# Two transformer layers on one core: attention output written straight to its place, inverses spread by the matmul engine, row maxima first in the DMA queue, and the output product kept behind the last value product

## The reference

```python
xn = layernorm(x)
x = x + attn0(xn) + swiglu_ffn(xn)        # 32 heads of 16, one shared K and V, no mask, biases
xn = layernorm(x)
x = x + attn1(xn) + lora_moe_ffn(xn)      # 32 heads of 16, 8 K/V heads, rotary, causal
# each attention:
scores = einsum('bqhd,bkhd->bhqk', q, k) / 4
out = einsum('bhqk,bkhd->bqhd', softmax(scores), v).reshape(B, N, 512)
return out @ Wo
```

## Time and profile before

| | |
|---|---|
| three runs, median (lowest, highest) | 2288.86 us (2284.86, 2290.49) |
| the profiled execution | 2291.59 us |
| its span in the trace | 2289.9 us |
| PE, DVE, ACT, POOL busy | 2002.2, 1434.8, 1090.0, 227.9 us |
| attention of layer 0, first to last value product | about 530 to 1293.8 us |
| from there to the end of layer 1's router products | 1293.8 to 1399.8 us |
| attention of layer 1, from its first maxima | 1570.7 to 2219.5 us |
| from there to the end | 2219.5 to 2289.9 us |

### The profile page before, as it was taken

The page is one execution under the profiler, slowest core; times in us unless marked ns, Lnnn a source line. Parts: engine busy times, 40 slices in busy tenths (PEclk is TensorE's granted clock), DMA queues, the critical chain, the costliest instruction groups (busy, mean ns, idle before and its releaser), DMA issues.

```text
span 2289.9 us, 28931 instructions
## 1 busy us (share of the span) xinstructions
PE 2002.2 (87%) x10608; PEld 990.4 (43%) x10608; DVE 1434.8 (63%) x1876; ACT 1090.0 (48%) x2150; POOL 227.9 (10%) x603
## 2 busy tenths in 40 slices
PE   3999999999999999999988868997888888886668
PEld 3878787633333333333332355444333333332216
DVE  7443445328888888888774183396666656664424
ACT  3221212234777777777664421142555555554460
POOL 4000000000000000000010030000231313131130
PEclk7999999997999999999896689996998989897889
DMA  5010100151121111113110211033111111112113
GB/s 171 14 42 0 38 0 0 38 149 31 28 50 30 27 44 34 30 33 84 27 48 3 66 46 51 19 104 86 26 30 40 37 32 36 34 44 61 47 47 113
DMA packets 83297, 105.19 MB, mean 46 GB/s; under 512 B 18816, under 2 KB 52608, under 8 KB 83168
## 3 DMA queue, kind: packets, MB, share of 16 engines
q1 hardware_dynamic: 83168, 103.49, 17.5%
HBM read 72.50 MB, written 30.15 MB: 45 GB/s over the span
## 4 chain that ended last, share of the span: by engine, by line
PE 68%; DVE 10%; ACT 8%; SPq 6%; DMA 5%; issue 2%; POOL 0%; DVEq 0%; POOLq 0%; ACTq 0%
PE ps L1165 17%; PE ps L1194 11%; ACT arena L666 6%; PE ps L955 6%; PE ps L956 6%; PE ps L957 6%; PE ps L1190 6%; PE ps L1112 5%; PE ps L1073 4%; PE ps L1118 3%; DMA slots<-arena 3%; PE ps L1029 2%; DVE arena L891 2%; SPq L353 2%; SPq L350 2%
## 5 line engine op out<-in xcount | busy, mean ns | idle before, releaser
L891 DVE TENSOR_REDUCE arena<-ps 128x1 f32<-128x1024 f32 (+7 forms) x1024 | 976.4, 988 | 323.1 <-PE ps L1115 225.8
L666 ACT ACTIVATE arena<-ps 128x512 f32<-128x512 f32 (+3 forms) x1792 | 874.2, 555 | 526.2 <-PE ps L1190 293.2
L1165 PE MATMUL ps<-arena 128*17 128x512 f32 (+3 forms) x3584 | 455.2, 581 | 22.5 <-ACT arena L657 21.9
L1194 PE MATMUL ps<-slots 50*128 50x512 f32 x1024 | 397.2, 473 | 29.7 <-ACT arena L666 10.9
L1118 PE MATMUL ps<-slots 48*128 48x512 f32 x1024 | 414.4, 484 | 8.1 <-DVE arena L891 7.2
L1194 PEld LDWEIGHTS ps<-slots 50*128 50x128 f32 x1024 | 177.5, 195 | 351.4 <-ACT arena L666 280.1
L1190 PE MATMUL ps<-slots 98*128 98x512 bf16 (+3 forms) x768 | 230.5, 356 | 87.9 <-DMA slots<-arena 84.6
L1112 PE MATMUL ps<-slots 96*128 96x512 bf16 (+3 forms) x768 | 231.9, 361 | 20.2 <-DVE arena L891 7.0
L955 PE MATMUL ps<-x_hi,w_hi 128*128 128x512 f32 (+1 forms) x480 | 195.4, 407 | 56.9 <-DVE x_lo L921 35.7
L1118 PEld LDWEIGHTS ps<-slots 48*128 48x128 f32 x1024 | 174.5, 195 | 60.5 <-DVE arena L891 34.2
L523 POOL TENSOR_SCALAR_AFFINE_SELECT arena<-arena 128x128 f32<-128x128 f32 x512 | 146.9, 294 | 497.8 <-ACT arena L666 486.2
(11 more groups left out here) (119 smaller groups left out, 1719.6 us busy)
## 6 DMA issues: line engine op xcount, KB each, us to landing
slots<-qparts SPq DMA_DIRECT2D x96, 128.0 KB, 3.6
qparts<-arena SPq DMA_DIRECT2D x32, 256.0 KB
numer<-arena SPq DMA_DIRECT2D x256, 32.0 KB
xnT<-numer SPq DMA_DIRECT2D x16, 512.0 KB
arena<-inverse SPq DMA_DIRECT2D x16, 512.0 KB
slots<-qparts SPq DMA_DIRECT2D x96, 64.0 KB, 3.4
qparts<-arena SPq DMA_DIRECT2D x48, 128.0 KB
slots<-qparts SPq DMA_DIRECT2D x32, 192.0 KB, 3.7
```

Of the source, the lines that this page charges most:

```text
L666: act.activation(prob[local % P_RING][:, q0:CH], bank(local % SP_RING)[:, q0:CH], ACT.Exp, scale=SCALE).then_inc(S["p_ready"], 1)
L891: dve.tensor_reduce(maxes[c][:, h * TPC + qt:h * TPC + qt + 1], src[:, 0:max_width(l == 1, c, qt)], AX_X, ALU.max).then_inc(S["x_done"], 1)
L1165: mm = pe.matmul(bank(7)[32 * h:32 * h + DH + 1, q0:CH], v_slot[n % SLOTS][:, kt, :], prob[idx % P_RING][:, q0:CH], start=(kt == 0), stop= ...
L1194: mm = pe.matmul(bank(slot)[:, q0:CH], k_slot[u][r:r + ROWS[0] + MROWS, kt * P:(kt + 1) * P].bitcast(F32R), q_slot[u][r:r + ROWS[0] + MROW ...
```

## The change

Attention's results no longer go through DRAM. `store_o` copies each head's sums from `o_sb` into their place in `xnT`, and the sums of exponentials into `inv`, 32 heads times 4 rows of 128: 8 DMAs in place of 5. `load_output` and `load_inverses` are gone. A constant `sel` of zeros and ones lets PE spread the inverses over the 16 rows of each head (`broadcast`: four float32 products of 32 rows by 128 columns for each of 4 blocks `k` of a chunk). For batch 0 the eight broadcasts, with a DVE product `xnT *= ps` for each, stand among the maxima of group 13 (`norms`); ACT makes `xo_hi` in group 14 and POOL `xo_lo` in groups 14 and 15. `wo_hi` is made by ACT in group 10, `wo_lo` by POOL at the start of group 11. SP sends the maxima's rows of chunk 1 ahead of `load_slot`. In layer 0's last group the 11 items left are spread over the first 0.42 of it.

The output product has a list, `tail_ring`: tiles 0 to 5, the four broadcasts of chunk 2, tiles 6 to 8, those of chunk 3, tiles 9 to 15, in four banks (3 to 6). `FIRST_PROJ = 99` means that none of its steps is taken inside `attend`: all come behind the last value product. DVE follows with `evac`, `moments` and `normalise` in the order below. Layer 1's projection weights are loaded in group 2 of layer 0, its feed-forward weights right after the last `store_o`.

```diff
+LAST_MAX_END = [0.42, 0.0]
+FIRST_PROJ = [99, 99]
+STEPS_PER_QUAD = 3
+    return tiles[0:6] + norms[2] + tiles[6:9] + norms[3] + tiles[9:TT]
...
             def store_o(l, n, c):
                 S = L[l]
                 sp.wait_ge(S["o_copied"], n * QC + c + 2)
+                b = n // NG
                 for h in range(HG):
-                    sp.dma_start(numer[l][n * HG + h:n * HG + h + 1, :, c * CH:(c + 1) * CH].rearrange("o d q -> (o d) q"),
+                    head = n % NG * HG + h
+                    r = head % (P // DH) * DH
+                    sp.dma_start(xnT[r:r + DH, head // (P // DH), b * N + c * CH:b * N + (c + 1) * CH],
                                  o_sb[c][32 * h:32 * h + DH, :]).then_inc(S["o_out"][c], 16)
-                sp.dma_start(denom[l][n * HG:(n + 1) * HG, c * CH:(c + 1) * CH],
-                             o_sb[c][DH:P:32, :]).then_inc(S["o_out"][c], 16)
+                    sp.dma_start(inv[head * TPC:(head + 1) * TPC, b * QC + c, :],
+                                 o_sb[c][32 * h + DH:32 * h + DH + 1, :].rearrange("o (a q) -> o a q", q=P)).then_inc(S["o_out"][c], 16)
...
-                    if n == GROUPS - 4:
-                        load_output(l, 0)
-                    if n == GROUPS - 2:
-                        load_inverses(l, 0)
-                    final = n == GROUPS - 1
+                    max_rows(l, u, 1, n * QC + 1)
                     if n + SLOTS - 1 < GROUPS:
                         sp.wait_ge(S["pv_done"], n * group_quads[l] + PQ)
                         load_slot(l, n + SLOTS - 1)
-                    max_rows(l, u, 1, n * QC + 1)
                     store_o(l, n, 0)
...
+                        if (n, c) == (GROUPS - 5, 0):
+                            pool.wait_ge(S["wo_hi_done"], KC)
+                            pool.tensor_tensor(wo_lo[:, :, :], w_o[:, :, :], wo_hi[:, :, :].bitcast(F32), ALU.subtract).then_inc(S["wo_ready"], 1)
...
+                dve.wait_ge(S["pv_done"], (GROUPS - 1) * group_quads[l] + PQ)
+                evac(0, 4)
+                chunk_moments(0)
+                evac(4, 6)
+                invert(2, 3, GROUPS)
+                norm(2)
+                low(2)
+                invert(3, 4, GROUPS)
+                evac(6, 9)
+                norm(3)
+                evac(9, 10)
+                low(3)
+                evac(10, 12)
+                chunk_moments(1)
+                if l == 0:
+                    normalise(1, 0)
+                chunk_moments(2)
+                if l == 0:
+                    normalise(1, 1)
+                evac(12, 16)
+                if l == 0:
+                    normalise(1, 2)
+                chunk_moments(3)
+                if l == 0:
+                    normalise(1, 3)
...
+                def broadcast(dst, c, k):
+
+                    rows = slice(32 * k, 32 * (k + 1))
+                    for a in range(TPC):
+                        mm = pe.matmul(dst[:, a * P:(a + 1) * P], sel[rows, a, :], inv[rows, c, :], start=True, stop=True,
+                                       tile_position=(32 * k, 0))
+                    return mm
...
-                            steps = [0] * len(todo)
+                            steps = [a * LAST_MAX_END[l] for a in pace(todo)]
+                            tail_at = 0
...
+                                if not has_next and h == BURST_AT and i_g > HG * FIRST_PROJ[l]:
```

More of the change, by code:

```diff
@@ L82, in max_blocks @@
         before = [(n - 1, 1, None, None)] if n else []
-        blocks.append(r[0][:2] + before + r[0][2:] + r[1][:2] + [(n, 0, None, None)] + r[1][2:])
+        norms = [(None, c, None, k) for c in range(QC) for k in range(KC)] if n == GROUPS - 2 else []
+        blocks.append(r[0][:2] + before + norms + r[0][2:] + r[1][:2] + [(n, 0, None, None)] + r[1][2:])
     blocks[-1].append((B * NG - 1, 1, None, None))
@@ L89, in max_width, with norms_through, tail_ring @@
     return (TPC * qc + qt + 1) * P if causal else N
+def norms_through():
+    items = [item for block in max_blocks() for item in block]
+    return items.index((None, QC - 1, None, KC - 1)) + 1
+def tail_ring():
+    norms = [[("norm", c, k) for k in range(KC)] for c in range(NCH)]
+    tiles = [("tile", t // TPC, t) for t in range(TT)]
+    return tiles[0:6] + norms[2] + tiles[6:9] + norms[3] + tiles[9:TT]
 def build(nc, x, wq0, bq0, wk0, bk0, wv0, bv0, wo0, bo0, wgu, wdn, wq1, wk1, wv1, wo1,
@@ L144, in build @@
             x_lo = fb("x_lo", [P, 2, KC, CH], F32R)
-            wo_hi, wo_lo = x_hi[:, 0, :, :], x_hi[:, 1, :, :]
-            xo_hi = w_hi[:, :, :].rearrange("p n f -> p (n f)")[:, 0:2 * KC * CH].rearrange("p (i k q) -> p i k q", i=2, k=KC)
-            xo_lo = x_lo
             xn0 = fb("xn0", [P, XN_RING[0], D])
@@ L161, in build @@
             slots1 = fb("slots1", [P, 2 * SLOTS * SLOT], BF16)
-        AR = 25 * 1024
+        XO = P_RING * CH + QC * CH + NCH * P
+        with ExitStack() as own:
+            fb("below_xo", [P, XO])
+            xo_hi = fb("xo_hi", [P, 2, KC, CH], F32R)
+            xo_lo = fb("xo_lo", [P, 2, KC, CH], F32R)
+        XN1 = XO + 4 * KC * CH
+        AR = 26 * 1024
+        with ExitStack() as own:
+            fb("below_wo", [P, AR - 2 * KC * D])
+            wo_hi = fb("wo_hi", [P, KC, D], F32R)
+            wo_lo = fb("wo_lo", [P, KC, D], F32R)
         arena = sb("arena", [P, AR])
@@ L211, in build @@
         o_sb = [region(CH) for _ in range(QC)]
[L212 to L216 removed]
+        inv = region(NCH * P).rearrange("p (c q) -> p c q", c=NCH)
+        assert used[0] == XO
         used[0] = PROJECTION + SLOTS * SLOT
@@ L515, in _, with low @@
                     stage_v(n)
+                def low(c):
+                    pool.wait_ge(S["xo_hi_done"], KC * (c + 1))
+                    pool.tensor_tensor(xo_lo[:, c % 2, :, :], xnT[:, :, c * CH:(c + 1) * CH], xo_hi[:, c % 2, :, :].bitcast(F32),
+                                       ALU.subtract).then_inc(S["xo_ready"], 1)
                 at = 0
@@ L583, in _ @@
                 else:
-                    for t in range(TT):
-                        act.wait_ge(S["hl_ready"], t + 1)
-                        act.activation(hl[:, t, :], bank(t % 2)[:, 0:E * R + E], ACT.Copy).then_inc(S["hl_sb"], 1)
                     act.wait_ge(S["gap_done"], 1)
@@ L678, in _ @@
                 attend()
[L681 to L689 removed]
+                for c in range(QC, NCH):
+                    for k in range(KC):
+                        xo_high(c, k)
+                    if l == 0 and c == QC:
                         deviation(1, 0)
@@ L735, in _ @@
                 dve.wait_ge(x_in[g], 16)
+                moments(0, g)
                 normalise(0, g)
@@ L1213, in _ @@
                     max_piece(*piece)
-                attend()
+                for step in range(attend(), steps_in_all):
+                    tail_step(step)
                 pe.wait_ge(S["o_copied"], GROUPS * QC + 1)
-                pe.wait_ge(S["wo_ready"], 1)
-                for t in range(TT):
-                    c, q = t // TPC, slice(t % TPC * P, (t % TPC + 1) * P)
-                    pe.wait_ge(S["xo_ready"], c + 1)
-                    if t >= 8:
-                        pe.wait_ge(S["y2_evac"], t - 7)
-                    for k in range(KC):
-                        last = passes(bank(t % 8), xo_hi[:, c % 2, k, q], xo_lo[:, c % 2, k, q], wo_hi[:, k, :], wo_lo[:, k, :], k == 0, k == KC - 1)
-                    last.then_inc(S["y2_ready"], 1)
 def kernel(**inputs):
```

303 lines of the change are left out of this document (181 added, 122 removed).

## The result

| | before | changed |
|---|---|---|
| median of the runs, us | 2286.86 (2283.43 to 2290.49) | 2198.43 (2188.06 to 2203.94) |
| profiled execution, us | 2291.59 | 2201.31 |
| its span, us | 2289.9 | 2199.4 |
| ratio to before | | 0.961, 95% interval 0.957 to 0.965 |

The change gains 88 us where 141 were forecast, and the median lies 8 us above the range. Three lines of the changed kernel's page: busy time, the clock in 40 slices, the chain by engine.

What follows compares the result with a forecast made beforehand. PE holds 68% of the chain, so its waits and low clock bound the kernel. Terms 100.0 - 13.4 + 15.4 + 3.7 + 23 + 12 = 140.7 off 2291.6 give 2150.9, as a median 2148 us; range 2115 to 2190.

Steps and rivals of the forecast that it cites:

- Rows first: Layer 1's attention: sending the maxima's rows ahead of the next slot's loads removes waits and lost clock, gaining 100.0 us.
- the two long waits: Layer 1, groups 12 and 14: PE's longest waits on the rows, with batch 0's reading back also queued; 17.18 us at 2165.09.
- the new wait: Layer 1, groups 1 to 14: PE's remaining wait on the rows, taken as 0.25 us each, bounds 0 to 0.8.
- the rows still come late: Rival: the store's new DMAs cost 0.85 each, PE waits 2.8 us again and the clock falls; 2203 us, chance 0.12.
- The additions in layer 1: Layer 1's attention: broadcasts 6 us, POOL's `wo_lo` 5, ACT's copies 1, longer last store 1.4; together -13.4 us.
- Layer 0, groups 12 to 14: Layer 0's attention: 17.4 us go, less 4.7 for clock, 6.5 for broadcasts and norms, 2.5 for copies; gain 3.7 us.
- The third rival: Layer 0: the inserted work starves PE and the clock is low through groups 13 to 15; 2163 us, chance 0.10.
- The reading back: Layer 0, groups 12 to 14: reading back batch 0 cost 17.4 us, forecast to go.
- The charge for the clock behind the reciprocal: Layer 0, ahead of group 12's maxima: the reciprocal stays and PE's low clock just behind it costs 4.7 us again.
- The last group: Layer 0's last group: spreading the 11 items left gains 23 us, with nine quads at low clock; bounds 12 to 38.
- the first rival: Layer 0's last group: the clock stays high, 15.6 us less, 2132 us; chance 0.20.
- The ends: After the last value products: layer 0 to the router's last product gains 12 us (6 to 20), layer 1's end 15.4.

Runs made afterwards that it cites:

- ends and rows: Changed kernel with batch 0's broadcasts at the head of each layer's end and layer 1's second-chunk rows ahead of the stores; 2136.9 us, 0.932 of the kernel before.

## Why the prediction was wrong, and where it was right

**Rows first (100.0).** The mechanism and the size of what was removed are right: the swap alone brings 82 us with the two long waits left in. Wrong is the new wait: "I take 0.25, too short to lower the clock", from stores at 0.46 us an issue, the mean of the old five. The new ones take 0.62 with the gaps between them (4.93 for eight; 0.51 to 0.54 for an output of 16 partitions, 0.62 to 0.65 for a row of sums, where the rows of the kernel before had 0.43 and 0.55), which makes the rows 1.2 us later than forecast. That is beyond the bound too, which put 0.57 on each (and comes to 0.65 us of wait by its own rows, not 0.8). PE waits 18.8 us in all and not 3.5, and clock goes with it: 31 us by the kernel that takes the stores out of the way. The rival "the rows still come late" was this mechanism, with 0.12 and a threshold of 0.85; it set in well below that.

**The additions in layer 1 (-13.4).** The broadcasts' group takes 14 us too long, where 6 were charged: a broadcast between scores takes 1.12 us at the high clock and not 0.9 (four in one go in the tail take 2.8, 0.7 each), and the clock falls in the middle of the eight (0.53 from 2033 on), after which each takes 2.07. The 5 us for POOL's low half, with ACT's copies of the weight, are seen as 4 where no waits hide them (33.8 and 33.9 us for groups 10 and 11 against 31.9).

**Layer 0, groups 12 to 14 (3.7).** This is the step that failed most: "PE has hardly any idle time in a regular group, so 6.5 (0 to 9)". The broadcasts cost 30.3 us between two transposes and 33.4 over three half groups, where 9 were charged with ACT's copies. The bounds were made from their own duration at the high clock. Nothing was asked about what their place in the list does: the pacing makes room for them by crowding the maxima, whose bound is VectorE (1.18 us each); this crowding alone is 11.7. And nothing was asked about the clock: it falls while they run, also without the crowding (10 us of low clock; both effects together 37), and each then takes 2.07. The third rival came near (0.10), with a low clock, but by a starved PE, which the rows do not show, and let it cost 15 us in all. The reading back is gone as forecast. The charge for the clock behind the reciprocal was right: 5.5 us (27.4 for the half group at 1040.36) for the 4.7 forecast, though in four of the other kernels' profiles the clock stayed high at that place and it cost 0.7. The half group in which ACT and POOL split the weight took 23.6 us, 1.7 more than a regular one (0.5 to 4.0 more in the other profiles), where the forecast had nothing.

**The last group (23).** Right: the last eighteen quads take 60.9 us instead of 80.9, with the clock low in the second half as I took it, 4.04 us a quad. The other level occurs too (2.59 a quad, 13 us less, in two other kernels' profiles), as the first rival had it. Nothing in the forecast decides between the two, so that the profile showed the low one was in part luck.

**The ends (12 and 15.4).** 18.5 and 12.4, together 3.5 us better than forecast; layer 0's lies inside its bounds. The listing's order held.

With 27 us for the stores (31 less 3.5) and 24 for layer 0's broadcasts the forecast comes to 2199; 8 more for layer 1's broadcasts are met by the rows' term, which was about 11 low: with both moves ("ends and rows"), layer 1's attention takes 495.5 us, 111 less than before, or 115 with the 4 for the weight's halves, where 103.5 had been reckoned. The range failed because both mishaps came together; either alone would have stayed inside it (about 2176 and 2172).

## What to carry to other kernels

When a DMA is pulled forward in a queue, look at everything still ahead of it: here eight stores that the same change had lengthened, behind which rows lay ready for 8 us. An item put into a paced list costs what it does to its neighbours and to the clock as well; ask which engine bounds them, and whether the item should carry weight at all. And if a change has one part that gives nearly all of it, measure that part alone first: here one swapped line alone gave 82 us, and the whole change 88.

## What the runs showed of the hardware

A busy engine is no guard of the clock. With broadcasts over 32 rows spread among other products, PE was busy for 61.2 of 63 us and had 0.50 all along, while the same stretch without them had 1.00 at 19.5 busy of 20. The Trainium skill (TensorE: Matmul & The Clock Gate, Part 1: The HAM clock gate) says that sustained activity releases the throttle; measured as PE's busy time, these rows don't agree. Eight broadcasts in one go brought the clock down as well, halfway through them (0.73 over the 11 us around them, PE busy for 10.95), but it was back within 5.5 us behind the last one, while the same eight among scores and crowded maxima had it low for 37 us. And the same half group with the same stop ahead of it ran at either level in different kernels, which makes 13 us; so did the stretch behind the reciprocal, which took 22.6 us in four kernels' profiles, 23.8 to 24.9 in five and 27.4 in three. This may be why executions of one kernel lie 5 to 27 us apart, though no run shows it.
